# Head 0 first: its attention operands copied inside SBUF, the router's products split around the first scores

## What is computed

```python
# attention, 16 heads of 8 dimensions, S = 2048
mod = cos(phase) * amplitude
q, k, v = (xn @ Wq) * mod, (xn @ Wk) * mod, (xn @ Wv) * mod
scores = q @ k.T / sqrt(8)
scores = scores * cos(2*pi*(i - j) / S)
w = softmax(scores)
w = (w + roll(w, 1, axis=-1)) / sqrt(2)
out = (w @ v) @ Wo
# router and experts: 8 experts, top 2, inner width 352
q, k, v = split(xn @ wqkv.T, 3)             # 8 values each
attn = softmax(q[..., :, None] * k[..., None, :])
logits = einsum('ej,j->e', attn, v)
top2, idx = top_k(logits, 2);  gates = softmax(top2)
out = sum over the 2 chosen e of gate * (silu(a) * g) @ w2[e].T,  [a, g] = xn @ w1[e].T
```

## Time and profile before

| what | us |
|---|---|
| median of 3 runs | 574.67 |
| lowest and highest | 573.45, 578.29 |
| the profiled execution, its own time | 575.55 |
| its span, first to last instruction | 573.8 |
| ACT busy | 513.2 |
| PE busy | 526.3 |
| DVE busy | 222.7 |
| POOL busy | 92.8 |

### The profile page before, as it was taken

How to read it: one execution, slowest core, us unless ns; L and a number is a source line. 1 busy time by engine, 2 the same in 40 slices (tenths; PEclk the granted TensorE clock), 3 DMA queues, 4 the chain that set the end, 5 groups by cost and what they waited for, 6 DMA issues and landing times.

```text
span 573.8 us, 19271 instructions
## 1 busy us (share of the span) xinstructions
PE 526.3 (92%) x7964; PEld 258.9 (45%) x7964; DVE 222.7 (39%) x521; ACT 513.2 (89%) x582; POOL 92.8 (16%) x102
## 2 busy tenths in 40 slices
PE   1978899979999999999999999999999999999884
PEld 1442333323334455455555545455554555455333
DVE  6876365615544332323323223332323131231234
ACT  2649999979999899989999999999999999999991
POOL 5210167531000101010101101010111101101000
PEclk9986999989999999999999999999999999999999
DMA  7962054371005252433415242432415233120222
GB/s 219 188 180 92 6 145 117 93 214 58 1 22 86 55 141 64 121 88 93 112 47 141 59 137 56 130 98 74 119 49 141 67 86 97 50 58 11 85 70 76
DMA packets 60891, 53.76 MB, mean 94 GB/s; under 512 B 33244, under 2 KB 50294, under 8 KB 60546
## 3 DMA queue, kind: packets, MB, share of 16 engines
q1 hardware_dynamic: 58082, 47.48, 31.5%
q0 software_dynamic: 2272, 4.72, 2.3%
q10 hardware_dynamic: 448, 0.30, 0.3%
HBM read 38.68 MB, written 13.78 MB: 91 GB/s over the span
## 4 chain that ended last, share of the span: by engine, by line
PE 59%; ACT 19%; issue 9%; DVE 8%; DMA 2%; SPq 2%; ACTq 0%; DVEq 0%
PE ps L1402 30%; ACT big L706 18%; PE ps L1381 12%; PE ps L1311 6%; PE ps L1324 4%; PE ps L1417 3%; DVE cs L995 2%; DVE m L1065 2%; PE ps L1200 2%; PE ps L1211 1%; DMA qk_parts<-store 1%; DVE store L789 1%; DMA acc<-in_L_attn_x 1%; PE ps L1351 1%; PE ps L1188 1%
## 5 line engine op out<-in xcount | busy, mean ns | idle before, releaser
L706 ACT ACTIVATE big<-ps 128x1024 f32<-128x1024 f32 x512 | 481.7, 1062 | 24.9 <-PE ps L1381 22.6
L1402 PE MATMUL ps<-big,vh 128*32 128x256 f32 (+1 forms) x3968 | 259.2, 393 | 0.4 <-ACT big L706 0.4
L1402 PEld LDWEIGHTS ps<-big,vh 128*32 128x32 f32 x3968 | 111.9, 110 | 114.5 <-issue 58.9
L1381 PE MATMUL ps<-qa,ka 49*128 49x512 f16 x896 | 142.2, 389 | 15.1 <-ACT big L706 9.2
L1381 PEld LDWEIGHTS ps<-qa,ka 49*128 49x128 f16 x896 | 34.7, 94 | 103.0 <-ACT big L706 72.0
L604 POOL DMA_INDIRECT results<-y,row_of x39 | 37.9, 973 | 254.1 <-DVE y L1001 253.0
L986 DVE SCALAR_TENSOR_TENSOR cs<-cs,ps 128x384 f32<-128x384 f32 x39 | 21.6, 554 | 113.7 <-ACT cs L698 113.7
L1311 PE MATMUL ps<-xgT,store 128*32 128x128 f32 x1716 | 65.2, 273 | 0.2
L1065 DVE TENSOR_REDUCE m<-ps 128x1 f32<-128x512 f32 x64 | 44.2, 691 | 54.5 <-PE ps L1417 54.5
L1311 PEld LDWEIGHTS ps<-xgT,store 128*32 128x32 f32 x1716 | 53.9, 110 | 14.1 <-issue 1.1
L621 POOL DMA_INDIRECT slots_x<-attnT,slot x32 | 35.7, 1116 | 53.2 <-PE ps L1402 49.8
(11 more groups left out here) (189 smaller groups left out, 212.4 us busy)
## 6 DMA issues: line engine op xcount, KB each, us to landing
store<-in_L_ffn_w SPq DMA_DIRECT2D x39, 352.0 KB, 3.1
store<-in_L_ffn_w SPq DMA_DIRECT2D x39, 192.0 KB, 3.3
qk_parts<-store SPq DMA_DIRECT2D x8, 512.0 KB, 4.1
qa<-qk_parts SPq DMA_DIRECT2D x27, 128.0 KB
slots_x<-vh SPq DMA_DIRECT2D x8, 330.0 KB, 7.1
cs<-slots_x SPq DMA_DIRECT2D x80, 32.0 KB, 2.6
store<-results SPq DMA_DIRECT2D x4, 512.0 KB, 5.7
ka<-qk_parts SPq DMA_DIRECT2D x31, 64.0 KB, 2.3
```

Source lines behind the costliest of these rows:

```text
L706: nc.scalar.activation(probs[:, prob_of(tiles[0]):prob_of(tiles[-1]) + 1, :], ps[:, bank_of(tiles[0]):bank_of(tiles[-1]) + 1, :], ACT.Exp, ...
L1381: ins = nc.tensor.matmul(ps[:, bank_of(n), :], k[at:at + KQ, P * o:P * o + P], q[at:at + KQ, CW * c:CW * c + CW], start=True, stop=True, t ...
L1402: ins = nc.tensor.matmul(ps[32 * c:32 * c + 32, O_BANK, cols], vh[:, p % 2, o + 8 * b, :], probs[:, prob_of(n), cols], start=k == 0, stop= ...
```

## The change

Head 0 is given the first place in every case: its bound is multiplied out to zero by a minimum with `heads * 1e30`, so that it ranks first. Since its number is known when the program is built, nothing waits for `head_order`: 12 DMAs copy its rows straight from `parts` to `qa[0]` and `ka[:, 0, :]`, inside SBUF, each as soon as its part is ready, and two more copy the shift's rows from the tile `shift`. Ten of the 12, and the shift's two, are issued by SP between the four stores; two by ACT, between `values(0)` and `values(1)`. ACT no longer issues four loads after `order_ready`. The values of head 0 are copied by POOL without the order.

The 16 router products, which stood together behind the last `values` and a wait for the shift, are now six ahead of `square_sums(0)`, four behind the last `values`, and six behind the scores of round 0. They are written 128 columns further on in the bank, and `turn_other(0)` uses another bank. The table load of ACT's exponential moves ahead of `values(3)`.

Eleven constants move work to later rounds, by two each, and `normalise(0)` by three quads; `EXPERTS_AT` stays, so that four of the 64 jobs of the exact heads move from the rounds before the experts to those beside them.

```diff
--- before.py
+++ after.py
@@ -74,25 +74,27 @@
 EXACT = 2
 PLAIN = H - EXACT
 JOBS = EXACT * NT * 2
-PAIR_EXP_AT = 0
-TOP_EXP_AT = 6
-RANK_AT = 6
-GATES_AT = 7
-SECOND_AT = 19
-JOBS_AT = 27
+PAIR_EXP_AT = 2
+TOP_EXP_AT = 8
+RANK_AT = 8
+GATES_AT = 9
+SECOND_AT = 21
+JOBS_AT = 29
 EXPERTS_AT = 45
 JOBS_BEFORE = 2 * (EXPERTS_AT - JOBS_AT)
 JOBS_BESIDE = JOBS - JOBS_BEFORE
 SCATTER_AT = 11
 ROUNDS_A_TILE = 3
 TURN_AT = EXPERTS_AT + ROUNDS_A_TILE * JOBS_BESIDE
-LATE_AT = 9
+LATE_AT = 11
 LATE = 2 * (16 - 12)
 ROTATIONS = 12 + LATE
-PARTS_AT = (12, 17)
-SQUARES_AT = (14, 18)
-STAGE_AT = 24
-FIRST_NORMALISED = 9
+PARTS_AT = (14, 19)
+SQUARES_AT = (16, 20)
+STAGE_AT = 26
+MIXED_FIRST = (6, 4)
+FIRST_LOADS = 14
+FIRST_NORMALISED = 12
 HALF_HEADS = H // 2
 EARLY = HALF_HEADS - EXACT
 EXACT_AT = TURN_AT + 1
@@ -281,6 +283,7 @@
             sem(n) for n in ("hidT_ready", "y_ready", "y_copied", "y_added"))
         staged_ld = [sem(f"staged_ld{i}") for i in range(STAGES)]
         aug_ld = [sem(f"aug_ld{i}") for i in range(2)]
+        first_ld = sem("first_ld")
         exact_ld, exact_shift_ld = sem("exact_ld"), sem("exact_shift_ld")
         score_ready, exp_done, pv_done, vh_ready = (sem(n) for n in ("score_ready", "exp_done", "pv_done", "vh_ready"))
         m_ready, m_reduced, mx_ready, mxT_ready, exact_shift_ready = (
@@ -401,6 +404,23 @@
             eng.dma_start(k[at + 1:at + 1 + 2 * ROWS, :], one(scratch[1, bass.ds(h, 1), :, :, cols])).then_inc(loaded, 16)
             eng.dma_start(k[at + 1 + 2 * ROWS:at + KQ, :], one(scratch[1, bass.ds(h, 1), 0:1, :, cols])).then_inc(loaded, 16)
 
+        def load_first(eng, part, which, halves):
+
+
+            rows = parts[0:P:ROWS // 2, which, part, :]
+            for half in halves:
+                to = (qa[0], ka[:, 0, :])[which]
+                cols = (slice(0, S), slice(HALF * half, HALF * half + HALF))[which]
+                for block in (((0, 1), (2,)), ((0, 2), (1,)))[which][part]:
+                    at = 64 * half + 1 + ROWS * block
+                    eng.dma_start(to[at:at + ROWS, :], rows[:, cols]).then_inc(first_ld, 16)
+
+        def load_first_shift(eng):
+            eng.wait_ge(shift_ready, 1)
+            for half in range(2):
+                eng.dma_start(qa[0][64 * half:64 * half + 1, :].rearrange("o (t p) -> o t p", p=P),
+                              shift[0:NT, 0, :]).then_inc(first_ld, 16)
+
         def run_again(eng):
 
             eng.wait_ge(again_ready, 1)
@@ -495,18 +515,16 @@
                              shift[:, g, :]).then_inc(shift_wr, 16)
 
             store_part(0, 0)
+            load_first(sp, 0, 0, range(2))
             store_part(1, 0)
             store_part(0, 1)
+            load_first(sp, 1, 0, range(2))
+            sp.wait_ge(rows_ready, 1)
+            load_first(sp, 0, 1, range(2))
             store_part(1, 1)
+            load_first_shift(sp)
             store_shifts(0)
             sp.wait_ge(scratch_wr, 4 * 16)
-            sp.wait_ge(rows_ready, 1)
-            sp.wait_ge(order_ready, 1)
-            h = sp.value_load(head_order[0:1, 0:1], min_val=0, max_val=H - 1)
-            load_operands(sp, h, qa[0], ka[:, 0, :], 0, aug_ld[0])
-            sp.wait_ge(shift_wr, 16)
-            for half in range(2):
-                load_shift(0, h, half)
             load_head(1)
             sp.wait_ge(wrap_ready, 1)
             sp.wait_ge(xt_ready, NC)
@@ -591,6 +609,9 @@
                 nc.gpsimd.tensor_tensor(paired_x[:, CW * c:CW * c + CW], xnT[:, CW * c:CW * c + CW], xnT[:, CW * c + 1:CW * c + CW + 1],
                                         ALU.add).then_inc(paired_ready, 1)
 
+            def first_values():
+                nc.gpsimd.tensor_copy(vh[:, 0, :, 0:D + 1], vaug[:, 0, :, :]).then_inc(vh_ready, 1)
+
             def head_values(p):
                 if p == EARLY:
                     pool.wait_ge(order_ready, 2)
@@ -607,8 +628,8 @@
             pool.wait_ge(v_ready, 4)
             pool.wait_ge(ones_ready, ONES)
             pool.wait_ge(zeros_wr, GROUPS * GROUP // 5 * 16)
+            first_values()
             pool.wait_ge(order_ready, 1)
-            head_values(0)
             head_values(1)
             nc.gpsimd.memset(qe_store[:], 0.0).then_inc(rows_ready, 1)
 
@@ -680,16 +701,14 @@
             square(1)
             act.wait_ge(ones_ready, ONES)
             values(0)
+            act.wait_ge(parts_ready, 2)
+            act.wait_ge(rows_ready, 1)
+            load_first(act, 1, 1, range(2))
             values(1)
             other_of_first()
-            act.wait_ge(order_ready, 1)
-            act.wait_ge(scratch_wr, 4 * 16)
-            act.wait_ge(rows_ready, 1)
-            h = act.value_load(head_order[0:1, 0:1], min_val=0, max_val=H - 1)
-            load_operands(act, h, qa[0], ka[:, 0, :], 1, aug_ld[0])
             values(2)
+            nc.scalar.activation(warm[:], ident[:, 0:1], ACT.Exp)
             values(3)
-            nc.scalar.activation(warm[:], ident[:, 0:1], ACT.Exp)
 
             def gate_of(m):
 
@@ -841,7 +860,7 @@
             def shifts(g):
 
                 dve.wait_ge(other_ps, g + 1)
-                nc.vector.tensor_scalar(shift[:, g, :], ps[:, SIDE_BANK, P:2 * P], -TO_SHIFT, None, ALU.mult).then_inc(shift_ready, 1)
+                nc.vector.tensor_scalar(shift[:, g, :], ps[:, FIRST_BANKS[g], P:2 * P], -TO_SHIFT, None, ALU.mult).then_inc(shift_ready, 1)
 
             def reach_of_heads():
 
@@ -856,7 +875,8 @@
             def take_reach():
 
                 dve.wait_ge(reach_ps, 1)
-                then(nc.vector.tensor_copy(rank[:, 0, :], ps[0:1, SIDE_BANK, 2:2 + H]))
+                dve.wait_ge(head_ld, 3 * 16)
+                then(nc.vector.scalar_tensor_tensor(rank[:, 0, :], heads[:], 1e30, ps[0:1, SIDE_BANK, 2:2 + H], ALU.mult, ALU.min))
 
             def place(n):
 
@@ -921,7 +941,7 @@
 
             def choose():
                 dve.wait_ge(mix_ps, 1)
-                then(nc.vector.tensor_copy(mix[:], ps[:, SIDE_BANK, 0:NT * 3 * E].rearrange("p (t n) -> p t n", t=NT)))
+                then(nc.vector.tensor_copy(mix[:], ps[:, SIDE_BANK, P:P + NT * 3 * E].rearrange("p (t n) -> p t n", t=NT)))
                 then(nc.vector.tensor_tensor(pair[:], over_j(mix[:, :, 0:E]), over_e(mix[:, :, E:2 * E]), ALU.mult))
                 then(nc.vector.tensor_reduce(gate[:, 0, :, :], pair[:], AX, ALU.max))
                 nc.vector.tensor_tensor(pair[:], pair[:], over_j(gate[:, 0, :, :]), ALU.subtract).then_inc(gexp_in, 1)
@@ -1236,7 +1256,7 @@
 
             def turn_other(g):
                 pe.wait_ge(other_ready, g + 1)
-                nc.tensor.transpose(ps[:, SIDE_BANK, P:2 * P],
+                nc.tensor.transpose(ps[:, FIRST_BANKS[g], P:2 * P],
                                     other[:, HALF_HEADS * g:HALF_HEADS * g + HALF_HEADS, :].rearrange("p h t -> p (h t)"),
                                     ident[:]).then_inc(other_ps, 1)
 
@@ -1253,7 +1273,7 @@
                 nc.tensor.matmul(ps[0:1, SIDE_BANK, 2:2 + H], reach[:, 2:3], of_head[:], start=True, stop=True).then_inc(reach_ps, 1)
 
             def mix_tokens(t):
-                ins = nc.tensor.matmul(ps[:, SIDE_BANK, 3 * E * t:3 * E * t + 3 * E], xnT[:, P * t:P * t + P], wqkvT[:], start=True, stop=True)
+                ins = nc.tensor.matmul(ps[:, SIDE_BANK, P + 3 * E * t:P + 3 * E * t + 3 * E], xnT[:, P * t:P * t + P], wqkvT[:], start=True, stop=True)
                 if t == NT - 1:
                     ins.then_inc(mix_ps, 1)
 
@@ -1283,6 +1303,8 @@
             rotate(8)
             rotate(9)
             rotate(10)
+            for t in range(MIXED_FIRST[0]):
+                mix_tokens(t)
             square_sums(0)
             for t in range(8, 12):
                 values(t)
@@ -1290,8 +1312,7 @@
             rotate(11)
             for t in range(12, NT):
                 values(t)
-            pe.wait_ge(shift_ready, 1)
-            for t in range(NT):
+            for t in range(MIXED_FIRST[0], sum(MIXED_FIRST)):
                 mix_tokens(t)
 
             def widen(m, b, ready):
@@ -1372,8 +1393,10 @@
                 after(pe, exp_done, g - GROUPS_A_ROUND + 1)
                 for n in group_tiles(g):
                     p, o, c, b = tile_at(n)
-                    if n % PER_HEAD == 0 and p < PLAIN:
-                        pe.wait_ge(aug_ld[p % 2], (p // 2 + 1) * 10 * 16)
+                    if n == 0:
+                        pe.wait_ge(first_ld, FIRST_LOADS * 16)
+                    elif n % PER_HEAD == 0 and p < PLAIN:
+                        pe.wait_ge(aug_ld[p % 2], (p + 1) // 2 * 10 * 16)
                     elif n % PER_HEAD == 0:
                         pe.wait_ge(exact_shift_ld, EXACT * 2 * 16)
                     q, k = operands(p)
@@ -1433,6 +1456,9 @@
                     max_job(j, expert_step(r)[0])
                 if r == TURN_AT:
                     turn_maxima()
+                if r == 0:
+                    for t in range(sum(MIXED_FIRST), NT):
```

(1 more changed line is left out.)

## The result

| | before | after |
|---|---|---|
| median, us | 574.22 (573.45 to 578.29, 4 runs) | 582.77 (581.46 to 585.23, 4 runs) |
| ratio | | 1.0136, 95% interval 1.0099 to 1.0173 |
| profiled execution, us | 575.55, span 573.8 | 582.16, span 580.4 |

The changed kernel is 1.4% slower. The forecast of 574.8 us and its range up to 578.0 were wrong.

A forecast was written before the change was run, and what follows sets the result against it. ACT was taken to set the pace once started, with time lost before its first exponential and at late scores. Terms -4.0 + 0 + 2.5 + 0.9 + 0.7 = +0.1 us gave 575.65 profiled, 574.8 median; 8-in-10 range 571.3 to 578.0.

The forecast's parts named there:

- The start: Up to ACT's first exponential: removed waits and DRAM round trip let it start at about 37.35 us, -4.0 us.
- the loads queue behind the stores: Rival, SP's queue at 32 to 37 us: costs 3.0 of the start's 4.0 us, giving 577.8 us; chance 0.12.
- The first rounds: First rounds after the start: router products hidden, clock falls as before, 0 us net, bounds -1.4 to +1.5.
- Clock stays up: Rival, first rounds: PE's granted clock does not fall, the stage gains 1.4 us, 573.4 us; chance 0.20.
- Round 23: PE's first product with head 2's values waits for DVE's bank copy behind the root steps, +2.5 us, at most +3.7.
- the clock falls too: Rival, new wait at round 23: the 2.5 us wait also makes the clock fall, giving 576.0 us; chance 0.12.
- The exact heads' operands: Ahead of the first job: normalising before the order lengthens PE's wait from 2.90 to 3.8 us, +0.9, between 0 and +1.5.
- Jobs: Four more expert tiles with a job, two rounds without jobs, and a moved turn: +0.7 us, between 0 and +1.5.
- slower by over 1%: Whole kernel above 580.4 us: needs no gain at the start and both waits with the clock; chance 0.04.
- new waits are hidden: Rival, both later waits: ACT's lead or shorter DVE work covers the 2.5 and 0.9 us, 571.4 us; chance 0.11.
- The change doesn't do what it says: Case at the start: copies do not come early at all, 578.8 us; counted within a rival's chance of 0.12.

The follow-up runs named there:

- e3: Changed kernel with SP copying q's parts, k's high part and the shift before three of the four stores; 582.61 us, 1.0100 of the kernel before.
- c1: The kernel before, unedited, run again on the third chip; 577.36 us, ratio 0.9983.
- e9: Changed kernel with bank copy and order_rest() earlier, three stores last, a load semaphore per exact head, and scatters five quads later; 567.31 us, ratio 0.9879.
- e10: Changed kernel with bank copy and order_rest() earlier, three stores last, a load semaphore per exact head, and head 2 loaded three rounds later; 568.66 us, ratio 0.9905.
- e2: Changed kernel with order_rest() directly behind shifts(1), ahead of normalise(1), on DVE; 585.49 us, 1.0139 of the kernel before.
- c0: The changed kernel, unedited, run again on the third chip; 591.64 us, 1.0252 of the kernel before.
- c2: The changed kernel, unedited, run again on the fifth chip; 587.93 us, 1.0153 of the kernel before.
- e11: Changed kernel with only the scatters five quads later (SCATTER_AT 16 for 11); 585.63 us, 1.0201 of the kernel before.
- e13: Changed kernel with seven of the eleven constants back to their old values, the router's four kept; 579.14 us, 1.0021 of the kernel before.

## Why the prediction was wrong, point by point

**The start, -4.0 us, was the step that failed.** It measured -0.7. The parts of the change that it names did go away: the wait for the stores, for the order, the round trip. The failure is in the sentence on SP: ten loads "issued" by the time the shift is ready, the last store between 32 and 33 us, and two shift DMAs at 33.4 and 34.0. I counted the ten at "up to 0.61 us each", the median of line 476. SP measured four stores of 3.0 us together, seven copies of 0.6 us, three of 1.5 and 0.5 us between them, with no wait anywhere: 24.04 + 3.0 + 4.2 + 4.5 + 0.5 = 36.2 us. With the three slow ones at 0.6 that is 33.5 (an estimate from these numbers), and the shift would have gone out when it was ready. I had the slow issue in view, 1.37 us as line 476's longest, and used it for the shift's two DMAs only, not for the ten in front of them. The other parts held: the shift was ready at 33.84 (33.35), its second copy landed after 2.91 us (2.8), and the first exponential came 0.78 us after the landing (0.78 at the lower clock).

The rival "the loads queue behind the stores" came nearest, with the start at 40.3 us; it measured 40.62. But its mechanism was the order of the transfers in flight, and what happened was the order of SP's issues: the shift's DMAs had not gone out. The ring order that the page DMA: Bandwidth & Descriptors of the Trainium skill describes, in its section on queues, rings and completion order, isn't needed for it. The runs don't rule it out as a smaller effect either: behind four stores the copies of the shift took 2.9 and 3.3 us to land, and in e3, with one store far ahead of them, 1.7 both. Counted from the first store, the shift's second copy landed 4.2 us sooner in e3 than after: 3.0 us by the earlier issue, 1.2 by the shorter landing. Nor were the landings of rows 4, behind no store as I said, on an empty queue: two loads of weights (352 and 192 KB) were issued just ahead of them, at 439.96 and 440.50 us.

**The first rounds, 0.** The bound of +1.5 us was right: the products did run at the lower clock, and the stage cost +0.5 net. Beside c1, which took 9.10 us for it with the kernel before, it would be +1.9, so the stage's own spread is larger than the term. What I took from rows 5, that the clock fell behind a run of tiny products and not in a rest, carried over in part: after the change it fell in a rest, at 38.0 us; in c1 it fell at 36.2 us, inside an unbroken run of router products (33.48 to 37.86 us); with the rest shortened it didn't fall in six profiles and fell in two, e9 and e10. "Clock stays up" was worth 1.9 us against the changed kernel. The rule of the page TensorE: Matmul & The Clock Gate of the Trainium skill, under what's actually happening, is that slow is the default and activity releases it. The fall at 38.0 us after the change and its absence in e3 agree with that; the falls in c1, e9 and e10, with PE busy in the records, do not fit it so simply.

**Round 23, +2.5 us, was right.** DVE's steps came within 0.4 us of the forecast (copy done at 111.26 against 111.3), PE's wait was 2.81, ACT's loss 2.96. That the clock falls too had 0.12; it was so in six of the seven profiles that have this wait, at up to 2 us more. The bound of +3.7 was too low for it: 5.1 in e2.

**The exact heads' operands, +0.9 us: the mechanism was right, the size off.** The normalising ahead of the order is the cause (e2 takes it away). From `shifts(1)` to the order's end 6.1 us went by, 6.2 forecast. But the wait was 4.61 us, not 3.8, as SP took 9.45 us to issue 16 loads (121.42 to 130.87) where it had taken 8.0; one issue of 1.56 us is most of that. With the fall of the clock, ACT's gap grew from 4.12 to 6.62 us: +2.5, above the upper end of +1.5.

**Jobs, +0.7 us, was right:** +0.87 beside the tiles of experts, less the forecast 0.3 for two rounds without jobs, which wasn't measured by itself.

Sum of what was measured: -0.7 + 0.5 + 3.0 + 2.5 + 0.6, and -0.5 in small parts and rounding, is the 5.4 us by which the last round starts later; 1.2 us behind the last round, where the clock fell, make it 6.6 in the profiled execution. The medians are 8.55 apart. The upper ends of my own bounds, -1.0 + 1.5 + 3.7 + 1.5 + 1.5 = +7.2, contained the 5.4. I treated them as independent of one another when I gave "slower by over 1%" a chance of 0.04; three of them are the same thing, a wait long enough for the clock to fall. It fell at two of the three places in the profile of after and at all three in c0, c2 and e11. With the three moved together the range would have reached 582, still 0.8 short of the median.

The other forecasts: "new waits are hidden" is refuted by all runs with the placement. "The change doesn't do what it says" is half true: e13, the start alone, is worth nothing that can be measured.

## What to carry to other kernels

A queue that issues DMAs in order is an engine with a timetable: count every issue on it, at the slow duration as well as the median, and put the transfer that the next stage waits for ahead of all that nobody waits for. Work that is moved by a few rounds meets, in an in-order engine, what is due in those rounds; list what stands behind it in the new round before choosing one (here a bank copy behind the root steps, an order behind a normalising, each mended by exchanging two blocks). And a wait of PE costs more than itself when the clock falls in it: a wait of 2.8 to 3.1 us cost ACT 3.0 without a fall and 4.5 to 5.1 with one (rounds 22 to 24, against 5.5). The same holds for comparing kernels: a fall in the last 17 us, where both kernels do the same work, moved the end by 1.2 to 3.7 us.
